# Attention stage of a cross-attention and expert kernel: token order, head moves, value store and value fetch rearranged

## What is computed

```
Q = (layernorm(x) @ Wq.T + bq).reshape(bs, sl, 16, 32)
K, V = (ctx @ Wk.T + bk), (ctx @ Wv.T + bv), reshaped alike
score = einsum("bshd,bsgd->bshg", Q, K)
weight = softmax(score, axis=-1)
attn = einsum("bshg,bsgd->bshd", weight, V)
x = x + attn @ Wo.T + bo
x = x + ffn(layernorm(x))
```

## Time and profile before

| what | value |
|---|---|
| median of 3 runs | 1547.17 us (1545.26 to 1549.24) |
| profiled execution | 1546.2 us, of which span 1544.5 us |
| PE / DVE / ACT / POOL busy | 88% / 58% / 46% / 24% of the span |
| mean granted clock of TensorE | 0.945 of full speed |
| transfers issued by SP for keys / queries / values fetched | 192 / 180 / 256 |

### The profile page before, as it was taken

How to read it: one execution, slowest core, us unless ns; L and a number is a source line. 1 busy time by engine, 2 the same in 40 slices (tenths; PEclk the granted TensorE clock), 3 DMA queues, 4 the chain that set the end, 5 groups by cost and what they waited for, 6 DMA issues and landing times.

```text
span 1544.5 us, 34518 instructions
## 1 busy us (share of the span) xinstructions
PE 1362.4 (88%) x11395; PEld 1021.2 (66%) x11412; DVE 898.0 (58%) x1952; ACT 715.4 (46%) x1500; POOL 369.4 (24%) x480
## 2 busy tenths in 40 slices
PE   5789888877777888758999999999999999999998
PEld 4668777766666777645666765666666666666775
DVE  6887777777777777765876554332222222333666
ACT  6376656666666666653225433333333333332221
POOL 4421111111111111000247711111111111113555
PEclk9898988999998899869999999999999999999999
DMA  5545555555555555576676452222222222225997
GB/s 191 131 120 160 162 161 148 162 165 165 165 166 142 148 158 163 144 250 235 205 122 107 60 127 91 82 83 85 83 81 81 81 81 82 83 79 183 294 316 236
DMA packets 263942, 223.22 MB, mean 145 GB/s; under 512 B 185046, under 2 KB 193310, under 8 KB 263535
## 3 DMA queue, kind: packets, MB, share of 16 engines
q1 hardware_dynamic: 243272, 178.63, 41.0%
q0 software_dynamic: 12880, 35.47, 7.7%
q10 hardware_dynamic: 7734, 8.40, 1.8%
HBM read 129.30 MB, written 67.96 MB: 128 GB/s over the span
## 4 chain that ended last, share of the span: by engine, by line
PE 47%; SPq 29%; DMA 8%; DVE 7%; issue 6%; ACT 2%; POOL 1%; POOLq 0%; DVEq 0%; ACTq 0%
PE psum_a L729 25%; PE psum_b L729 18%; SPq L489 14%; SPq L519 10%; DMA value_rows<-heads 7%; PE psum_b L1019 2%; PE psum_b L1041 1%; DVE d_m L1708 1%; DVE wdn L1794 1%; DVE gate_act L1683 1%; DMA wgu_in<-expert_rows,pos_ix 1%; DMA heads<-in_wk_t 1%; DVE sh_t L1689 1%; SPq L480 1%; SPq L557 1%
## 5 line engine op out<-in xcount | busy, mean ns | idle before, releaser
L729 PE MATMUL psum_a<-wgu,zg_t 128*128 x1704 | 266.1, 313 | 2.1 <-DVE zg_t L1805 1.7
L729 PEld LDWEIGHTS psum_a<-wgu,zg_t 128*128 128x128 f16 x1704 | 165.5, 98 | 89.2 <-issue 10.3
L1087 ACT ACTIVATE at_raw<-psum_a 32x128 f32<-32x128 f32 x384 | 147.8, 385 | 54.5 <-PE psum_a L729 49.9
L729 PE MATMUL psum_a<-zt_in,wsgu 128*128 128x256 f16 x1536 | 170.8, 273 | 0.9 <-ACT y_sb L1310 0.8
L729 PEld LDWEIGHTS psum_a<-zt_in,wsgu 128*128 128x128 f16 x1536 | 149.0, 98 | 24.8 <-issue 6.6
L2028 POOL DMA_INDIRECT zg<-z_rows,gather_ix x71 | 67.2, 946 | 407.5 <-DVE gather_ix L1801 400.4
L1915 POOL TENSOR_SCALAR var_eps<-mv 128x1 f32<-128x1 f32 x64 | 22.8, 356 | 548.4 <-DVE mv L1375 390.3
L1810 DVE SCALAR_TENSOR_TENSOR silu<-psum_a,w_scale,silu 128x352 f32<-128x352 f32 x71 | 41.5, 584 | 189.4 <-ACT silu L1297 189.4
L729 PE MATMUL psum_b<-wdn,act_t 128*128 (+1 forms) x639 | 149.6, 379 | 1.6 <-DVE act_t L1817 1.6
L729 PE MATMUL psum_b<-wsdn,sh_t 128*128 128x512 f16 (+1 forms) x576 | 134.7, 388 | 17.4 <-DVE sh_t L1689 16.5
L1297 ACT ACTIVATE silu<-psum_a,w_scale 128x352 f32<-128x352 f32 x71 | 39.3, 553 | 200.9 <-PE psum_a L729 200.9
(11 more groups left out here) (247 smaller groups left out, 2395.6 us busy)
## 6 DMA issues: line engine op xcount, KB each, us to landing
expert_rows<-y_sb SPq DMA_DIRECT2D x71, 256.0 KB
k_st<-k_parts SPq DMA_DIRECT2D x192, 64.0 KB, 2.1
q_st<-q_parts SPq DMA_DIRECT2D x180, 64.0 KB, 2.1
wgu_in<-in_wgu_t SPq DMA_DIRECT2D x8, 1408.0 KB, 16.6
x_sb<-in_x SPq DMA_DIRECT2D x16, 512.0 KB, 4.1
cx_in<-in_ctx_t SPq DMA_DIRECT2D x16, 512.0 KB, 7.0
x_res<-in_x SPq DMA_DIRECT2D x16, 512.0 KB, 5.4
value_rows<-heads SPq DMA_DIRECT2D x16, 512.0 KB, 7.4
```

The costliest lines, as they stand in the source:

```text
L729: return nc.tensor.matmul(o, l, r, start=start, stop=stop)
L1087: return nc.scalar.activation(o, i_, ACT.Copy)
```

## The change

1. A token's place: the queries, keys and sums of a block are laid out so that the 8 residues of the token number modulo 8 go across the whole block of 256 tokens (partition = residue, column = token / 8). ScalarE does the permutation when it reads the projections out of PSUM (`split_heads`), and `sums_out` undoes it.
2. `q_st`, `k_st`, `q_parts`, `k_parts` have 4 groups of 64 columns instead of 8 of 32. The 24 transfers of `move_heads` stay 24 of 64 KB; their runs are 512 bytes instead of 256. The scores read with a column step of 64 bytes instead of 32.
3. `fetch_values` leaves SP and goes to the start of GpSimd's pass, as 8 transfers of 64 KB in 512 runs of 128 bytes each (source), with the same waits for the store and for P1 of the pass before.
4. `store_values` stands right behind `move_queries` in SP's list.
5. ScalarE: `weights_out(1)` before `z_out`. VectorE: `add_attended` for half 0 before the second softmax, for half 1 right behind it; `logits_out` and `z_low(1)` ahead of `weigh_context`; `weigh_piece` at the end.

```diff
-        q_st = sb("q_st", [ROWS, NJ, H, PAIR * NG], F16, one)
+        q_st = sb("q_st", [ROWS, NB32, H, SUB * NG * PAIR], F16, one)
...
-        q_parts = sb("q_parts", [P, 2, NJ, KC, PAIR * NG], F16, one)
+        q_parts = sb("q_parts", [P, 2, NB32, KC, SUB * NG * PAIR], F16, one)
...
-                dst = at_raw[:, :, s * P:(s + 1) * P].rearrange("p c (t j q) -> p q c j t", q=4, t=GT)[:, q]
+                dst = at_raw[:, :, s * P:(s + 1) * P].rearrange("p c (j q t) -> p q c j t", q=4, t=GT)[:, q]
...
             def body(i, behind, ahead, ahead3, rows_from=None):
-                fetch_values(i)
                 if rows_from is not None:
                     load_piece(i, rows_from)
                 if ahead:
...
                     move_queries(i)
+                    store_values(i)
...
                     store_columns(i)
-                if ahead:
-                    store_values(i)
...
-                        q_side, k_side = (st[:, s * NB32 + b].rearrange("p h (t g) -> p (h t) g", g=NG)[:, :, g] for st in (q_st, k_st))
+                        q_side, k_side = (st[:, b].rearrange("p h (t n) -> p (h t) n", t=PAIR)[:, :, s * NG + g] for st in (q_st, k_st))
...
-                    pe.wait_ge(v_moved, (i + 1) * (SUB * GT * 16))
+                    pe.wait_ge(v_moved, (i + 1) * (GT * 16))
...
-                    src = bank_ap(step)[:, c * BT:(c + 1) * BT]
-                    nc.scalar.activation(whole_[:, 2 * b + c, :], src, ACT.Identity,
+                    src = bank_ap(step)[:, c * BT:(c + 1) * BT].rearrange("p (n b t) -> p b t n", b=NB32, t=PAIR)
+                    nc.scalar.activation(whole_[:, 2 * b + c, :].rearrange("p (b t n) -> p b t n", b=NB32, t=PAIR), src, ACT.Identity,
...
                 weights_out(0, i)
+                weights_out(1, i)
                 if behind:
                     z_out(i)
-                weights_out(1, i)
...
+                if behind:
+                    add_attended(i, (0,))
                 softmax(i, 1)
+                if behind:
+                    add_attended(i, (1,))
                 if ahead2:
                     wait_full(dve, "X1", i)
                     normalise_x(i + 2)
                 if behind:
-                    add_attended(i)
-                if behind:
                     normalise_out(i)
-                if weighs:
-                    weigh_piece(i, weighs)
...
                 if behind:
                     z_low(i, 0)
+                    logits_out(i)
+                    z_low(i, 1)
                 if ahead2:
                     weigh_context(i + 2)
                 if ahead:
                     spread_context()
-                if behind:
-                    logits_out(i)
-                    z_low(i, 1)
+                if weighs:
+                    weigh_piece(i, weighs)
...
+            def fetch_values(i):
+                pool.wait_ge(v_stored, (i + 1) * 16)
+                settle(pool)
+                if not (isinstance(i, int) and i == 0):
+                    wait_full(pool, "P1", i - 1)
+                    settle(pool)
+                src = v_d[bass.ds(i * BT, BT), :].rearrange("(n t) (h d) -> t h n d", t=GT, h=H)
+                for t in range(GT):
+                    at = t // PAIR * HD + t % PAIR
+                    pool.dma_start(v_p[at:at + HD - t % PAIR:PAIR, :, :], src[t]).then_inc(v_moved, 16)
...
             def body(i, behind, ahead2):
+                fetch_values(i)
```

More of the change, by code:

```diff
@@ L53 @@
 ROWS = 3 * HD + PAIR
-NJ = BT // (PAIR * NG)
 HI, LO = 0, 1
@@ L205, in build @@
         weigh_in = sb("weigh_in", [P, PIECE], F32, one)
-        q_st = sb("q_st", [ROWS, NJ, H, PAIR * NG], F16, one)
-        k_st = sb("k_st", [ROWS, NJ, H, PAIR * NG], F16, one)
+        q_st = sb("q_st", [ROWS, NB32, H, SUB * NG * PAIR], F16, one)
+        k_st = sb("k_st", [ROWS, NB32, H, SUB * NG * PAIR], F16, one)
         heads = sb("heads", [P, 2, KC, BT], F32, one)
@@ L211, in build @@
         v_rows = q_whole.rearrange("p c t -> p (c t)").rearrange("p (s d) -> p s d", s=SUB)
-        q_parts = sb("q_parts", [P, 2, NJ, KC, PAIR * NG], F16, one)
-        k_parts = sb("k_parts", [P, 2, NJ, KC, PAIR * NG], F16, one)
+        q_parts = sb("q_parts", [P, 2, NB32, KC, SUB * NG * PAIR], F16, one)
+        k_parts = sb("k_parts", [P, 2, NB32, KC, SUB * NG * PAIR], F16, one)
         v_p = sb("v_p", [P, SUB * NG, HD], F32, one)
@@ L506, in store_values @@
                 sp.dma_start(rows(v_d, i + 1), v_rows).then_inc(v_stored, 16)
[L508 to L519, removed]
             def load_cx(i):
@@ L1091, in split_heads @@
                 for c in range(2):
-                    src = bank_ap(step)[:, c * BT:(c + 1) * BT]
-                    nc.scalar.activation(whole_[:, 2 * b + c, :], src, ACT.Identity,
+                    src = bank_ap(step)[:, c * BT:(c + 1) * BT].rearrange("p (n b t) -> p b t n", b=NB32, t=PAIR)
+                    nc.scalar.activation(whole_[:, 2 * b + c, :].rearrange("p (b t n) -> p b t n", b=NB32, t=PAIR), src, ACT.Identity,
                                          bias=bias[:, 2 * b + c:2 * b + c + 1], scale=scale)
-                    last = nc.scalar.activation(parts[:, HI, :, 2 * b + c, :], src.rearrange("p (j t) -> p j t", j=NJ), ACT.Identity,
+                    last = nc.scalar.activation(parts[:, HI, :, 2 * b + c, :].rearrange("p b (t n) -> p b t n", t=PAIR), src, ACT.Identity,
                                                 bias=bias[:, 2 * b + c:2 * b + c + 1], scale=scale)
@@ L1197, in _ @@
             for rows_below, factor, size in ((copy8[0], ident[0:PAIR, 0:PAIR], MASK_Q), (copy8[1], other[:, :], 1.0)):
-                nc.scalar.activation(rows_below.rearrange("p j h (t q) -> p (j h) t q", t=PAIR), factor.unsqueeze(1).unsqueeze(3).broadcast_to([PAIR, NJ * H, PAIR, NG]),
+                nc.scalar.activation(rows_below.rearrange("p b h (t n) -> p (b h) t n", t=PAIR), factor.unsqueeze(1).unsqueeze(3).broadcast_to([PAIR, NB32 * H, PAIR, SUB * NG]),
                                      ACT.Copy, scale=size).then_inc(mask_ready, 1)
@@ L1385, in low_heads @@
                 hi, lo = (parts[:, part, :, 2 * b:2 * b + 2, :].rearrange("p j c t -> p c j t") for part in (HI, LO))
-                V.tensor_tensor(lo, whole_[:, 2 * b:2 * b + 2, :].rearrange("p c (j t) -> p c j t", j=NJ), hi, ALU.subtract).then_inc(done, 1)
+                V.tensor_tensor(lo, whole_[:, 2 * b:2 * b + 2, :].rearrange("p c (j t) -> p c j t", j=NB32), hi, ALU.subtract).then_inc(done, 1)
             def values_out(i):
@@ L1506, in split_attended, with add_attended @@
                     low(V, lo, raw, hi).then_inc(at_split, 1)
-            def add_attended(i):
+            def add_attended(i, subs=range(SUB)):
                 dve.wait_ge(x1_stored, i * 16)
-                for s in range(SUB):
+                for s in subs:
                     wait_full(dve, f"O{s}", i)
```

## The result

The changed kernel takes 1450.01 us, median of 4 runs (1449.22 to 1453.02); the kernel before, run beside it, 1547.38 us (4 runs, 1545.26 to 1549.24). The ratio is 0.9375, 95% interval 0.9356 to 0.9393. The profiled execution spans 1449.1 us against 1544.5: 95.4 us less.

What follows compares the result with a forecast made beforehand. SP's issuing was taken to bound the 40.7 us pass, then a ScalarE-VectorE-TensorE loop of 37.0 us. 13 passes gave 48 us, plus 2 at the start and 8 in the last pass: 58 less, 1489 us, range 1457 to 1540.

Steps and rivals of the forecast that it cites:

- One sign: On SP: its 24 head moves would no longer be end to end, and SP would wait for S1 or q_low.
- Rival C: GpSimd generates the fetch run by run, 4.5 us a transfer: pass 49.1 us, 1646 us in all; chance 0.14.
- the price of 3.1 us: GpSimd's cost per fetch transfer by a straight line through two profile rows; gave a pass of 39.1 us, 1516 us.
- the direct row: Lower bound for one GpSimd fetch transfer: a direct transfer of 71 rows holds GpSimd for 622 ns.
- the middle between the two ends: GpSimd's price per fetch transfer, taken as 2.0 us, about midway between the direct row and the line's 3.1 us.
- a fetch of 17.6 us: GpSimd's whole fetch: 8 transfers of 2.2 us with spacing; plus 11.5 us a loop of 29 us, hidden.
- 21.3 + 1.2: VectorE from scores to z_low: 21.3 us of work plus two assumed 0.6 us waits beside GpSimd, bounds 0 and 4.
- the terms taken as zero: ScalarE's strided PSUM reads (up to +6 us), quicker sums copies (up to -2), scores' column step (0 to 2.5), DMA engines.
- 2.9 us from `route` to the copies: In the loop, from TensorE's `route` start to ScalarE's start on the next sums: 2.9 us a pass.
- rival A: TensorE at full clock once the pause before `route` vanishes, no VectorE waits: pass 34.7 us, 1459 us; chance 0.08.
- PE's own 32.9 us: TensorE's busy time in a pass, said to lie below the 35.8 us loop, so near but not deciding.
- Rival B: Shared port: VectorE's two casts each wait for a whole GpSimd transfer, 4 us; pass 39.8 us, 1525 us.

Runs made afterwards that it cites:

- the fetch in 48: The changed kernel with GpSimd's value fetch cut into 48 transfers instead of 8: 1576.44 us, ratio 1.0169.
- e4_strided_sums: The changed kernel with the copies of the weighted sums writing with the old 64-byte step between neighbouring tokens (wrong columns): 1477.99 us, ratio 0.9535.
- e9_old_lists_strided: The changed kernel with ScalarE's and VectorE's old lists and the old 64-byte write step together (wrong columns): 1510.8 us, ratio 0.9741.
- run 426: Not a run label: 426 ns is the middle cast length over the whole run of the changed kernel with its fetch in 48 transfers, 1576.44 us.
- the first experiment: The kernel before with only its 16 value transfers issued by GpSimd instead of SP, all else old: 1510.45 us, ratio 0.9731.
- e3_old_lists: The changed kernel with ScalarE's and VectorE's orders as they were before: 1457.5 us, ratio 0.9393.
- e7_less_v: The changed kernel without the third product of the V projection, 16 matmuls instead of 24: 1458.14 us, ratio 0.9392.

## Why the prediction was right in sign and wrong in size

**What was right.** SP's issuing set the pass, and it left the chain when the fetch left SP. The start, the last pass and the unchanged feed-forward part came out as forecast within 3 us. One sign was badly chosen: SP's 24 moves still run end to end (332.59 + 7.71 against 340.41); what shows SP free is that it waits some 8 us a pass for TensorE's scores ahead of them. Rival C (GpSimd generates run by run, slower) and the price of 3.1 us were wrong by the row above: 631 ns. The price is nearly all per transfer; six times the runs, and the bytes with them, add 0.1 us. The bound from below, the direct row, was the true price, and the middle between the two ends that I took was three times too high. It did no harm to the sum, because a fetch of 17.6 us, with the 12 to 13 us that the fetch in 48 had beside it, would have been hidden too (an estimate; no run has such a fetch).

**The sum, term by term.** The loop closes in each kernel; each column is one pass, from scores to scores, worked out from the starts in its timeline (the last two are e4_strided_sums and e9_old_lists_strided):

| us | forecast | changed kernel | old write step | old step and lists |
|---|---|---|---|---|
| copies of the sums | 9.55 | 6.77 | 9.66 | 9.61 |
| x_out to the scores | 1.9 | 2.07 | 1.83 | 1.83 |
| VectorE, scores to z_low | 21.3 + 1.2 | 23.39 | 22.54 | 24.37 |
| z_low to `route` | 0.1 | 0.14 | 0.14 | 0.13 |
| `route` to the copies | 2.9 | 1.57 | 1.57 | 2.85 |
| sum | 37.0 | 33.94 | 35.74 | 38.79 |

The failed steps are these:
- The copies: "if the sums' now contiguous writes are quicker the 9.55 us shrink by up to 2" stood among the terms taken as zero, and there it stayed. They shrank by 2.8, past the bound, which was drawn from no row. It is the largest miss: put back, it costs 1.75 us a pass net, 25 us in all by the ratios (0.9535 against 0.9375).
- The clock. 2.9 us from `route` to the copies were read from a pass at half clock there, and kept. In the changed kernel the place runs at 2.4 GHz, 1.3 us less. That was rival A's reason, at a chance of 0.08. A and the sum both looked at the pause before `route` (5.76 us) alone, though; what goes with the clock is told under the open points. A's 34.7 us and 1459 us came near the result partly by luck: A had neither the faster copies nor the next point, and its condition was not the right one.
- VectorE's stretch was 23.4, not 21.3 + 1.2 = 22.5. The 1.2 us were for waits between VectorE and GpSimd; the 2.1 us are others. In the pass shown in the first section (other rows of the same timeline) VectorE waits 0.49 us for ScalarE's q_parts, 0.72 for its z_parts, 0.37 for TensorE's output projection and 0.37 for results of its own. ScalarE in turn waited 2.24 and 0.86 us for TensorE's Q ahead of q_parts: TensorE has become nearly as slow as the loop. I had written "PE's own 32.9 us lie below it, so PE is near but doesn't decide"; with the loop shorter than foreseen, both meet at 34 us.

The page "DMA: Bandwidth & Descriptors" of the Trainium skill, section "Issuing engines are not separate DMA queues", calls what another issuing engine saves usually small beside the transfer. Both of this case's numbers stand beside that: 42 us of 1547 when SP issued 16 transfers for this fetch, 7 to 14 us when it issues 8. Rival B, VectorE's casts held up by the fetch, had 0.17 and 1516 us. The changed kernel can't test it: its fetch ends at 359.33 us and the next cast starts at 362.99. The kernel with the fetch in 48 can. There the casts at 351.64 and 352.71 lie inside the fetch and last 0.43 us each, over the whole run 426 ns in the middle and 475 at most, against 420 and 427 in the kernel before. So casts beside GpSimd's transfers don't wait for them, and B falls. The Trainium skill ("SBUF — State Buffer", section "SBUF: two separate sides") states a lock by which, in some modes of VectorE, either engine fully blocks the other. These casts show no such block; whether they run in such a mode no run shows.

**What the sign rests on.** By the ratios, 42 of the 97 us come from the new issuing engine, the other 55 from the lists and the write step together: lists first 32 and step 25, or step first 54 and lists 3, because they overlap. The diff's store place, run length in head moves and number of transfers bring nothing that these runs can see, given the other parts.

**What is open.** What exactly tips the clock at `route` wasn't isolated, but the timelines narrow it down. Here are two neighbouring passes of the first experiment:

```profile
344.02 0.63 PE L773 MATMUL psum_b<-ident,z 128*128 128x128 f32 x4 [1.40 <-DVE z L1509]
346.03 0.63 PE L773 MATMUL psum_b<-ident,z 128*128 128x128 f32 x4 [1.38 <-DVE z L1509]
349.47 1.08 PE L715 MATMUL psum_b<-z_t,wgate 128*32 128x256 f32 x8 [2.81 <-DVE z_parts L1462]
...
383.40 1.32 PE L773 MATMUL psum_b<-ident,z 128*128 128x128 f32 x8
387.40 0.64 PE L715 MATMUL psum_b<-z_t,wgate 128*32 128x256 f32 x8 [2.68 <-DVE z_parts L1462]
```

The pause right before `route` is nearly the same, 2.81 and 2.68 us. In the first pass TensorE had also paused before each half of z, and `route` runs at half clock; in the second both halves ran as one, and `route` runs at full clock. The kernel before has such a pass too: z as one, a pause of 3.55 us, and `route` at 153.67 us lasts 0.64. e3_old_lists waits only before `route` (2.6 us a pass) and has it at full clock in every pass; e7_less_v pauses at z in every pass and has it at half clock in 12 of 13. With the old write step both occur. So it goes with the pauses at z, not with the one before `route` alone.

## What to carry to other kernels

When a change takes the binding engine away, sum the next loop with everything that the change does to it, the small edits above all: a better write step hid behind SP before, and was worth some 25 us once SP was gone. Look at which clock a TensorE duration was read; if the change removes the pauses that go with the half clock, price it at full clock, and if it makes new ones, the other way round. And where TensorE, VectorE and ScalarE meet within a microsecond, taking work from one gains nothing.

## What was unexpected of the hardware

- Issuing cost goes by transfers, hardly by their runs or bytes: GpSimd 530, 564 and 631 ns for about 85, 256 and 512 runs; SP 584 ns for 512.
- A PSUM-to-SBUF copy of 32x128 values costs ScalarE 381 ns with a 64-byte write step and 268 side by side, VectorE 379 and 291. A strided PSUM read by ScalarE cost nothing: the activations that write `heads` are 567 to 572 ns, as before (572 to 573).
- Removing 1.8 us of matmuls from a pass lowered TensorE's granted clock from 1.00 to 0.93 in its neighbourhood (200 to 404 us), and the pass was no shorter (34.39 against 33.97 us).
- The clock at `route` went with TensorE's pauses at z, not with the pause before `route`: with it 2.68 us long but z in one piece `route` lasted 0.64 us, with 2.81 and two pauses of 1.4 us at z 1.08.
